# Gates of four experts through TensorE in the first and the last group of a fused macaron block

## The reference

```python
x = x + 0.5 * _L0_ffn_ref(_layernorm(x), router_w, w1, w2)
x = x + _L0_attn_ref(_layernorm(x), W_qkv, W_out)
x = x + 0.5 * _L0_ffn_ref(_layernorm(x), router_w, w1, w2)
```

## Time and profile before

| | |
|---|---|
| median of 3 runs | 799.12 us (795.67 to 800.61) |
| profiled execution | 802.07 us |
| its span, first to last instruction | 800.3 us |
| PE / PEld busy | 727.1 us (91%) / 590.2 us (74%) |
| POOL busy | 686.3 us (86%) |
| ACT / DVE busy | 597.6 us (75%) / 581.4 us (73%) |
| mean granted TensorE clock | 0.974 |

### The profile page before, as it was taken

The page is one execution under the profiler, slowest core; times in us unless marked ns, Lnnn a source line. Parts: engine busy times, 40 slices in busy tenths (PEclk is TensorE's granted clock), DMA queues, the critical chain, the costliest instruction groups (busy, mean ns, idle before and its releaser), DMA issues.

```text
span 800.3 us, 13031 instructions
## 1 busy us (share of the span) xinstructions
PE 727.1 (91%) x3600; PEld 590.2 (74%) x3600; DVE 581.4 (73%) x1832; ACT 597.6 (75%) x1219; POOL 686.3 (86%) x668
## 2 busy tenths in 40 slices
PE   1788788889999999999999999999999987979977
PEld 1566566667888888888888888888887866767755
DVE  3456688777879798878778786978686768577533
ACT  3577677658888879888888888797878766656755
POOL 3778867869999999999999999999999858666875
PEclk9999999989999999999999999999999989989999
DMA  5553023023323311322333233322223311303230
GB/s 178 185 162 131 19 88 106 1 106 107 106 107 120 106 76 63 128 82 107 119 107 120 107 121 106 120 89 91 69 100 105 120 50 57 120 2 119 119 120 26
DMA packets 31159, 79.36 MB, mean 99 GB/s; under 512 B 3312, under 2 KB 14448, under 8 KB 31088
## 3 DMA queue, kind: packets, MB, share of 16 engines
q1 hardware_dynamic: 30800, 78.47, 28.7%
q10 hardware_dynamic: 288, 0.07, 0.1%
HBM read 73.81 MB, written 4.72 MB: 98 GB/s over the span
## 4 chain that ended last, share of the span: by engine, by line
PE 32%; DVE 28%; POOL 13%; issue 13%; ACT 10%; DMA 3%; DVEq 1%; POOLq 0%; ACTq 0%; SPq 0%
DVE hid L1033 7%; POOL h_lo L866 6%; PE bank L508 4%; PE bank L528 4%; POOL root_f L860 4%; PE bank L529 4%; PE bank L530 4%; PE bank L510 4%; PE bank L509 4%; ACT h_hi L738 2%; DVE pick_f L1011 2%; PE bank L597 2%; DMA g_all_f<-rows_f 2%; PE bank L489 2%; POOL x_lo_at L854 2%
## 5 line engine op out<-in xcount | busy, mean ns | idle before, releaser
L866 POOL TENSOR_TENSOR h_lo<-hid,h_hi 128x512 fp32r<-128x512 f32 x384 | 492.9, 1308 | 77.0 <-ACT h_hi L738 76.4
L1033 DVE SCALAR_TENSOR_TENSOR hid<-bank,g_all_f 128x512 f32<-128x512 f32 x384 | 262.2, 684 | 141.5 <-PE bank L510 101.1
L727 ACT ACTIVATE hid<-hid 128x512 f32<-128x512 f32 x384 | 228.7, 621 | 51.8 <-DVE hid L1033 51.7
L738 ACT ACTIVATE h_hi<-hid 128x512 fp32r<-128x512 f32 x384 | 225.6, 620 | 4.9 <-PE bank L530 0.4
L508 PE MATMUL bank<-x_hi_f,w_hi 128*128 128x512 f32 x384 | 166.4, 433 | 15.2 <-DVE hid L1033 15.1
L528 PE MATMUL bank<-h_hi,w_hi 128*128 128x512 f32 x384 | 157.4, 410 | 10.8 <-POOL h_lo L866 10.8
L510 PE MATMUL bank<-x_hi_f,w_lo 128*128 128x512 f32 x384 | 154.7, 403 | 0.0
L529 PE MATMUL bank<-h_lo,w_hi 128*128 128x512 f32 x384 | 154.3, 402 | 0.0
L530 PE MATMUL bank<-h_hi,w_lo 128*128 128x512 f32 x384 | 153.8, 400 | 0.0
L509 PE MATMUL bank<-x_lo_f,w_hi 128*128 128x512 f32 x384 | 153.7, 400 | 0.0
L508 PEld LDWEIGHTS bank<-x_hi_f,w_hi 128*128 128x128 f32 x384 | 74.1, 193 | 40.4 <-DVE hid L1033 24.5
(11 more groups left out here) (102 smaller groups left out, 1019.1 us busy)
## 6 DMA issues: line engine op xcount, KB each, us to landing
g_all_f<-rows_f SPq DMA_DIRECT2D x128, 512.0 KB, 5.5
x_sb<-in_x SPq DMA_DIRECT2D x16, 256.0 KB, 3.3
out_x<-x_sb SPq DMA_DIRECT2D x16, 256.0 KB, 7.0
g_all_f<-in_w SPq DMA_DIRECT2D x2, 768.0 KB, 6.7
con<-in_const SPq DMA_DIRECT2D x1, 584.0 KB, 6.2
rows_f<-g_row_f SPq DMA_DIRECT2D x32, 16.0 KB, 1.4
g_all_f<-in_wqkv SPq DMA_DIRECT2D x1, 192.0 KB, 6.4
con<-in_const ACTq DMA_DIRECT2D x1, 68.0 KB, 3.1
```

Of the source, the lines that this page charges most:

```text
L727: fn(h, h, ACT.Square).then_inc(s_sq[s], 1)
L738: fn(h_hi[:, c, :], hid[:, c % STAGE, :], ACT.Copy).then_inc(s_hhi[s], 1)
L866: gp.tensor_tensor(h_lo[:, c, :], hid[:, c % STAGE, :], h_hi[:, c, :].bitcast(F32), ALU.subtract).then_inc(s_hlo[s], 1)
L1033: v.scalar_tensor_tensor(hid[:, c % STAGE, :], hp[c % 2][:], 0.0, g_all[s][:, EXPERT[c], :], ALU.max, ALU.mult).then_inc(s_z[s], 1)
```

## The change

`NOW = 4`. For two groups only, f1's group 0 and f2's group 15, the gates of experts 0 to 3 no longer go through DRAM. PE multiplies each gate column of `g_tok`, broadcast to a 128x128 stationary operand, with the identity, four matmuls of 128 columns for each expert, 16 in all; the result in a PSUM bank holds the gates of the 512 tokens in every partition. The banks are a0, a1, a2 and for the fourth expert an unused output bank (f1) or `tp` (f2), which PE takes only when ACT has cut `g_row` out of it. ACT copies each bank to `g_all` with the same relu and cut. SP leaves out pieces 0 and 1 of these two groups. Pieces 2 and 3 still go through DRAM.

In the first iterations three steps move: ACT rounds w1 behind `exp_logits("f1", 0)` rather than ahead of group 0's `evacuate_x`; DVE makes `w1_lo` behind `choose_two` of group 0; POOL makes `inv_std("f1", 1)` behind `root_of_weights("f1", 0)` rather than ahead of it.

```diff
+        def at_once(s, n):
+            return not isinstance(n, Step) and (s, n) in (("f1", 0), ("f2", NG - 1))
+        def gate_bank(s, e):
+            return [a0, a1, a2, yp["f1" if y_bank("f1", 0) is yp["f2"] else "f2"] if s == "f1" else tp][e]
+        def sent(s, k):
+            return 1 if s == "f1" and PIECES[k][1] <= NOW else 0
...
                 for k, (e0, e1) in enumerate(PIECES):
+                    if at_once(s, n) and e1 <= NOW:
+                        continue
...
+            def gates_at_once(s, n):
+                if not at_once(s, n):
+                    return
+                pe.wait_ge(s_gt[s], value(n + 1))
+                for e in range(NOW):
+                    if gate_bank(s, e) is tp:
+                        pe.wait_ge(s_gr[s], value(n + 1))
+                    for k in range(TG):
+                        i = mm(gate_bank(s, e)[:, k * P:(k + 1) * P], g_tok[s][:, e, k:k + 1].to_broadcast([P, P]), ident,
+                               start=True, stop=True)
+                    i.then_inc(s_gp[s], 1)
...
                 weight_rows("f2", t + 1 - SHIFT, t, 1)
+                gates_at_once("f2", t + 1 - SHIFT)
...
                 weight_rows("f1", t + 2, t, 4)
+                gates_at_once("f1", t + 2)
...
+            def gates_at_once(s, n):
+                if not at_once(s, n):
+                    return
+                if due(n):
+                    act.wait_ge(s_z[s], n * NC - (NC - NOW))
+                for e in range(NOW):
+                    act.wait_ge(s_gp[s], e + 1)
+                    fn(g_all[s][:, e, :], gate_bank(s, e)[:], ACT.Relu, bias=c_cut[:, 0:1]).then_inc(s_gc[s], 1)
...
                 exp_logits("f1", t + 2)
+                if first_time(True, t + 2):
+                    act.wait_ge(s_w1, 16)
+                    fn(w1_hi[:], w1_raw, ACT.Copy).then_inc(s_w1hi, 1)
...
                 rows_of_weights("f2", n2)
+                gates_at_once("f2", n2)
...
                 rows_of_weights("f1", t + 2)
-                if first_time(True, t + 3):
-                    act.wait_ge(s_w1, 16)
-                    fn(w1_hi[:], w1_raw, ACT.Copy).then_inc(s_w1hi, 1)
+                gates_at_once("f1", t + 2)
                 if first_time(True, t + 2):
                     act.wait_ge(s_w2, 16)
...
-                inv_std("f1", t + 3)
+                if not first_time(True, t + 2):
+                    inv_std("f1", t + 3)
                 remainders(t, 2, 3, 4, 5, 6)
                 root_of_weights("f1", t + 2)
+                if first_time(True, t + 2):
+                    inv_std("f1", t + 3)
...
+                    if at_once(s, n) and EXPERT[c] < NOW:
+                        dve.wait_ge(s_gc[s], EXPERT[c] + 1)
+                    elif c in PIECE_FROM:
+                        k = PIECE_FROM.index(c)
+                        dve.wait_ge(s_ga[s][k], value((n - sent(s, k)) * 16 + 16))
...
-                if first_time(True, t + 3):
-                    split_w1()
...
                 choose_two("f1", n1)
+                if first_time(True, n1):
+                    split_w1()
```

More of the change, by code:

```diff
@@ L54 @@
 TOPK = 2
+NOW = 4
 PAD = 96
@@ L305, in build @@
         s_gt = per("gt", FFN)
+        s_gp = per("gp", FFN)
+        s_gc = per("gc", FFN)
         s_ct = per("ct", FFN)
@@ L390, in broadcast @@
                 if due(n):
-                    for arrived in s_ga[s]:
-                        sp.wait_ge(arrived, read)
-                        sp.sem_inc(s_gate_sp, 1)
+                    for k, arrived in enumerate(s_ga[s]):
+                        if due(n - sent(s, k)):
+                            sp.wait_ge(arrived, read - 16 * sent(s, k))
+                            sp.sem_inc(s_gate_sp, 1)
                 sp.dma_start(rows[s].rearrange("e (k p) -> (e k) p", k=TG), g_row[s][:]).then_inc(s_gd[s], 16)
@@ L1022, in weighted @@
                 for s, n, c, ago in chunks(t, place):
-                    if c in PIECE_FROM:
-                        dve.wait_ge(s_ga[s][PIECE_FROM.index(c)], value(n * 16 + 16))
+                    if at_once(s, n) and EXPERT[c] < NOW:
[3 more added lines that the diff above has]
+                        dve.wait_ge(s_ga[s][k], value((n - sent(s, k)) * 16 + 16))
                     m = n * NC + (c - STAGE + 1)
```

## The result

| | before | after |
|---|---|---|
| median, 6 runs each | 798.93 us (795.67 to 800.61) | 806.35 us (804.69 to 807.17) |
| ratio after / before, 95% interval | | 1.0093 (1.007 to 1.0117) |
| profiled execution, its span | 802.07 us, 800.3 us | 806.73 us, 804.9 us |

The change costs 7.4 us, where 2.3 were forecast (the median of before is 799.12 us over its first three runs and 798.93 over six). 806.35 lies 0.35 us outside the range. The forecast's sign was right. The two profiled executions lie only 4.6 us apart (spans of 800.3 and 804.9), while the medians lie 7.4 us apart: the profiled execution of before, at 802.07 us, was slower than each of its six measured runs.

The account below looks back on a forecast made before the run. PE's chunks bound the middle, POOL close behind; a chain through DRAM to POOL's first h_lo sets the start. Span 800.3 + 3.5 (start) - 1.2 (end) = 802.6; on the median 799.1 + 2.3 = 801.4 us, range 796 to 806.

Parts of the forecast that it names:

- nothing gained: Start up to g_tok: moving w1_lo frees DVE 1.76 us, but g_tok comes as before, PE's transpose at 19.77.
- norm ahead of g_row: Start, ACT: norm of group 1 waits for the moved inv_std, so g_row goes from 20.21 to about 22.4.
- The matmuls, 5.8 us: Start, PE: gate matmuls from 20.0 to 25.8, 20 instructions at the lower clock level, 12 at the upper.
- C: Rival: upper clock level from the beginning, start +1.8, end -1.2, 799.7 us; chance 0.1.
- D: Rival: step-0 operand or PSUM copies are dear, start +4.8 or more, end +2.3, 806.2 us; chance 0.06.
- w2_hi behind the fourth copy, w2_lo in front of low_part: Start, ACT and POOL: w2_hi ends at 27.8, w2_lo at 31.3, then low_part, first h_lo at 32.6.
- the start's term, +3.5: POOL's first h_lo at 32.6 instead of 29.10, group 1's root at 40.2 instead of 36.67: 3.5 us later.
- the shift is carried on: Middle: the start's delay persists, since gaps up to about 80 us wait for the same chain.
- End: -1.2 us: Last group: DVE's c0 0.6 us sooner and no lower-clock stretch on PE, DVE's c11 at 789.0, 1.2 us gained.
- the rival of tail_only: Follow-up's rival: about 3 us lost at the end with its lower clock, also in before's profiled execution; 799 to 801.
- B: Rival: the start's shift dies out through slack between POOL's first h_lo and 100 us, 797.9 us; chance 0.2.
- E: Rival: a real win, DVE starts at once in both places, 5.5 + 5.3 us, 788.3 us; chance 0.04.

Follow-up runs that it names:

- pick_only: Kernel before plus one wait: for f1's groups 1 to 4 POOL waits behind the root until DVE has made pick; 795.62 us, ratio 0.9971.
- inv_only: Kernel before with only group 1's inverse root on POOL moved behind group 0's root, all gates through DRAM; 800.62 us, ratio 1.0027.
- w1_only: Kernel before with only w1's rounding on ACT and w1_lo on DVE moved, all gates through DRAM; 799.73 us, ratio 1.0013.
- tail_only: Kernel before with only the last group's four gates through TensorE, start and three moves as before; 800.41 us, ratio 1.0006.
- start_gates_no_moves: Kernel before with only the first group's four gates through TensorE, the three moves taken back; 803.07 us, ratio 1.0057.
- start_only: Changed kernel with the last group's gates back through DRAM; first group's gates through TensorE and the three moves kept; 805.38 us, ratio 1.0076.

## Why the prediction was wrong, point by point

**Up to g_tok: "nothing gained", and g_tok "comes as before". Failed.** The step was to let w1_lo on DVE and the root on POOL run side by side at no cost, as if different engines could not hold each other up. In all five kernels with w1_lo moved they exclude each other: the one that starts second waits for the whole of the first, and the trace shows its wait as duration and not as idle time. g_tok came 1.64 us late (transpose at 21.41 instead of 19.77). The trace of before had a sign of this in it. The view by source of two DVE lines of before (duration in ns, min/median/max):

```profile
L951 DVE CAST x_hi_f<-xT x32: 410/726/1517, 13.7 to 751.3; 128x512 fp32r<-128x512 f32 x32
...
L1011 DVE TENSOR_TENSOR pick_f<-chosen_f,root_f x32: 207/748/1306, 19.2 to 761.4; 128x64 f32<-128x64 f32 x32
```

The longest case of each lies 1.1 us above its shortest, nearly the length of one h_lo or low_part on POOL (1.28 us). A spread like this in an instruction of fixed shape is a hint that it waits inside its row; pick_only confirmed it for pick. The Trainium skill (SBUF — State Buffer, Who interferes with whom) says that DVE and GpSimd share one port pair, that a DVE instruction with two SBUF inputs, or a cast that runs in a 2-port mode, contends with a GpSimd instruction that reads SBUF, and that whichever starts first has it for the whole instruction. The runs agree in each case: 3.15 to 3.23 us for the root against 1.63, 3.29 for the cast against 0.42, 1.27 for pick against 0.23; the mode in which the cast runs stands in no trace. By that section of the Trainium skill the step would have been priced right beforehand.

**norm ahead of g_row, price 2.2 us. Right.** inv_only gives g_row at 22.23 (forecast 22.4). In the changed kernel the stretched root adds its 1.6, hence 24.11. There it wasn't what decided: the third and the fourth copy waited for PE's matmuls (25.87 and 26.76).

**The matmuls, 5.8 us, with the rise of the clock during them. Right in kind, 0.7 too long.** They took 5.12 us here, 5.53, 5.56 and 6.36 in the other kernels: it depends on when TensorE rises, and all values lie between the bounds of 3.55 and 6.9. At the upper level 24 instructions took 2.84 us and 16 took 1.95, so each more costs 0.111, as in L628; a stationary operand with step 0 costs nothing more. Rivals C and D are out.

**w2_hi behind the fourth copy, w2_lo in front of low_part. Right, and undersized.** w2_lo ended at 32.3 rather than 31.3. What was missed is that it also held the cast to x_hi (until 32.63), which on DVE stands in front of c1, and c1's square in front of c0's h_hi. The first h_lo could have stood behind w2_lo and low_part at 33.6; low_part came 0.4 us late for want of the cast, and h_lo then waited 0.50 for ACT, until 34.49, 0.9 us more. The prediction had ACT a microsecond ahead of POOL there.

So the start's term, +3.5, measured +5.4: 1.6 from the root, less 0.7 of matmuls, and 0.9 from the cast are 1.8 of the 1.9 between them.

**Middle: "the shift is carried on" and "the matmuls and copies cost nothing there". Failed in part.** The shift of the changed kernel's roots against before is 5.39 us at group 1, 4.30 at group 2, 5.11 at group 3, 4.1 from 117 to 428 us, 5.05 from 494 to 581, 6.5 from 641 to 705 and 5.67 at the last root. Three things move it.

First, the way from group 1's g_row through DRAM to DVE's first chunk took 7.54 us before and 6.43 in the changed kernel, which is the 1.1 us that go between group 1 and group 2. In the twelve profiled executions it took 6.0 to 8.1 us; in w1_only, at 6.31, it took back 1.2 of its 1.4 us. Whether a kernel's timing or chance decides it isn't shown.

Second, TensorE stands still in the changed kernel in two places where before it did not, with nothing in the profile that it waits for ("issue"):

```profile
478.20 0.47 PE L539 MATMUL bank<-x_hi_f,w_hi 128*128 128x512 f32 x1 [0.80 <-issue]
...
610.30 0.47 PE L539 MATMUL bank<-x_hi_f,w_hi 128*128 128x512 f32 x1 [0.96 <-issue]
```

Behind each of them the shift is 1.2 us larger. The first stands in all four kernels with the first group's gates through TensorE, at 477 to 479 us and with a step of 1.2 us each time, and in none of the eight others. The second stands in the changed kernel alone. So the change has a price in the middle that the prediction put at nothing. Its cause is open; that it comes with the instructions that were added for the first group is all that the traces show.

Third, there are steps that are not the change's: in w1_only a step of 1.6 us, forward, lies at 164 to 189 and one of 2.1 at 641 to 674. The windows view of these two stretches (stretch, length, busy of PE, PEld, DVE, ACT, POOL, clock, DMA, GB/s), first w1_only, then before:

```profile
164.00:189.00 25.00, 20.57 (x109) 16.50 (x108) 19.14 (x59) 20.23 (x45) 19.05 (x21) 1.00 0.30 99
641.00:674.00 33.00, 26.45 (x141) 21.11 (x139) 25.33 (x76) 22.92 (x46) 24.91 (x29) 1.00 0.19 65
```

```profile
164.00:189.00 25.00, 20.91 (x99) 16.83 (x98) 19.03 (x59) 18.65 (x42) 17.43 (x20) 0.92 0.23 78
641.00:674.00 33.00, 28.70 (x144) 23.59 (x143) 23.46 (x73) 21.54 (x43) 22.99 (x25) 0.90 0.20 65
```

In both stretches the granted clock fell in one execution and not in the other. In the first, 99 recorded matmuls were done instead of 109 where it fell; in the second the counts are nearly alike (144 and 141), but they kept PE busy for 28.70 us instead of 26.45. Over all twelve executions the second step goes with the clock of 641 to 674: at 1.00 (three) a kernel gains 2.1 us against before there, at 0.95 (three) 0.7 to 1.1, at 0.90 (six, before among them) nothing. Steps of this kind are large enough to make up most of the 5 us between runs of one kernel; run by run that isn't shown.

**End: -1.2 us. Failed, though PE's side of it came true.** PE's hold was 4.14 us (forecast 4.1), c0 10.0 us behind the transpose (9.8), the end 35.8 us (35.7). What failed is the other side of the difference, 36.9 us, taken from one execution. Through DRAM the end has no fixed length. In eight profiled executions of kernels with the last gates through DRAM it took 34.0, 34.0, 34.4, 34.4, 35.8, 36.9, 37.3 and 38.7 us, 35.7 in the mean. The change puts 35.8 in its place, in both of its executions (changed kernel and tail_only): no gain. Two rows show a part of the spread, the wait for the first piece, of start_gates_no_moves (end 34.0 us) and of w1_only (38.7):

```profile
774.47 1.29 DVE L1081 SCALAR_TENSOR_TENSOR hid<-bank,g_all_f 128x512 f32<-128x512 f32 x2 [3.97 <-DMA g_all_f<-rows_f]
```

```profile
770.18 1.29 DVE L1081 SCALAR_TENSOR_TENSOR hid<-bank,g_all_f 128x512 f32<-128x512 f32 x2 [5.88 <-DMA g_all_f<-rows_f]
```

The first piece lands 9.1 us behind the transpose in the one and 11.0 in the other, 1.9 of the 4.7 us. The granted clock goes with the rest: from 773 to 776 us, just behind the wait, it is 0.50 in w1_only, while in start_gates_no_moves it stays at 1.00 up to 793. So the rival of tail_only was right in that the lower level makes the end slow; but it comes in some executions only, and the profiled one of before had it (0.54 from 776 to 779).

**The sum.** The start measured +5.4 instead of +3.5, and the end nothing instead of -1.2: together 3.1 of the 4.95 us between 801.4 and 806.35. The rest belongs to the middle, which the prediction put at nothing. In the profiled executions it holds two stops of TensorE worth 1.2 us each and a landing that was 1.1 us shorter, so 5.4 + 2.4 - 1.1 = 6.7 us, against 7.4 measured (interval 5.6 to 9.3). That start_only has only the first of the two stops fits its smaller loss (1.0076 x 799, 6.1 us), but these are single executions, and neither the second stop nor the last 0.7 us is settled by them.

**The range and the rivals.** None of the five rivals was the missing one. The range stopped short of a start of +5 us or more, which only D had and for another reason. B, that the shift dies out, is refuted for the changed kernel by the root marks (5.67 us at the last one), and its place by the rows: TensorE is back at the lower level at 35.19, with 0.63 us for 512 columns. A shift can vanish, though, as in w1_only, by the landing of the next group's gates. E is refuted by DVE's wait of 5.59 us for PE at 27.97.

## What to carry to other kernels

DVE and POOL are not two free engines here: before moving a DVE instruction with two SBUF inputs, or a cast, look at what POOL does at that moment, and read a spread in the durations of one instruction as the hint of a wait. A gain at a DMA wait should be counted against several executions, since the landing and TensorE's clock behind the wait made up a spread (34.0 to 38.7 us) larger than the gain. Work handed to the in-order engine that feeds the critical chain pays its whole length, so give it only as much as fits its slack: two experts gained 2.5 us where four gained nothing. And a change of the first group alone can cost time in the middle: compare the gaps of the busiest engine there as well.

## What the runs showed of the hardware that was not expected

- A POOL instruction on 128x8 elements lasted 3.15 to 3.23 us, twice its 1.63, when a DVE instruction with two SBUF inputs had begun 0.03 to 0.09 us ahead of it. A DVE cast lasted 3.29 us instead of 0.42 behind a POOL subtraction of 3.44 us that had begun 0.44 us earlier.
- A wait of 0.3 us for POOL, added to the kernel, took 1.04 us off pick and about 2.1 us off the kernel's chain, 0.9 of them by a shorter way through DRAM.
- TensorE stopped for 0.80 to 0.83 us at 477 to 479 us, with no releaser in the profile, in all four kernels that had 32 more matmul instructions at 20 to 28 us, and in none of the eight others; each time the roots behind it came 1.2 us later.
- The granted clock column of before stood at 1.00 up to 27 us, while the matmuls of 512 columns between 22.0 and 24.2 us lasted 0.63 us, as long as those at 28.5 to 30.3, where the column says 0.50. Their durations, not the column, told the level of 1.2 GHz, and the gate matmuls' 5.1 to 6.4 us agree with them: at the upper level they would have taken 3.6.
